# Attention: row maxima turned on VectorE, softmax totals inverted and spread by DMA, head outputs put in the last layer's order by DMA

## The reference

```
xd      = layernorm(x) @ W_down                      # 8 x 1024 x 256
keys, queries, values = per-head 16x16 products of xd, keys and queries scaled
attn    = softmax(queries @ keys^T over all 1024 keys)
out     = x + (attn @ values) @ W_unify + b_unify
```

## Time and profile before

| | |
|---|---|
| median of 3 runs | 2914.65 us |
| profiled execution, its own time / span | 2909.2 / 2907.5 us |
| TensorE busy (matmul) | 94% |
| VectorE / ScalarE / GpSimd busy | 74% / 63% / 21% |
| attention | about 640 to 2280 us of the span |
| mean granted TensorE clock | 0.968 of full |

### The profile page before, as it was taken

The page is one execution under the profiler, slowest core; times in us unless marked ns, Lnnn a source line. Parts: engine busy times, 40 slices in busy tenths (PEclk is TensorE's granted clock), DMA queues, the critical chain, the costliest instruction groups (busy, mean ns, idle before and its releaser), DMA issues. The chain is left out here.

```text
span 2907.5 us, 48802 instructions
## 1 busy us (share of the span) xinstructions
PE 2719.2 (94%) x17073; PEld 1648.7 (57%) x17073; DVE 2138.9 (74%) x3424; ACT 1838.3 (63%) x3473; POOL 600.8 (21%) x562
## 2 busy tenths in 40 slices
PE   5899999967999999999999999999999579999997
PEld 4799998853334334333343343333433369999886
DVE  6655456647899888898998988888896565554674
ACT  5444455633777777777777777777777444444564
POOL 3354114521100101001001001010000145421353
PEclk9899999977999999999999999999999899999998
DMA  5211113414123132131231321312210512111342
GB/s 171 66 43 49 52 52 104 137 51 79 24 52 70 32 61 52 38 61 36 48 74 32 58 55 29 70 36 43 51 41 2 161 39 80 49 43 43 97 135 66
DMA packets 159666, 180.66 MB, mean 62 GB/s; under 512 B 31816, under 2 KB 129296, under 8 KB 159504
## 3 DMA queue, kind: packets, MB, share of 16 engines
q1 hardware_dynamic: 151312, 167.99, 23.6%
q0 software_dynamic: 8192, 10.57, 1.2%
HBM read 96.46 MB, written 30.49 MB: 44 GB/s over the span
## 5 line engine op out<-in xcount | busy, mean ns | idle before, releaser
L1524 DVE TENSOR_REDUCE at_mxc<-at_pb 128x2 f32<-128x1024 f32 x1024 | 1219.6, 1219 | 157.7 <-PE at_pb L1341 150.0
L1454 ACT ACTIVATE at_ex<-at_pd 128x512 f32<-128x512 f32 x2048 | 1091.3, 599 | 361.6 <-PE at_pd L1352 355.1
L768 DVE TENSOR_TENSOR f_ml_hl<-f_ml_h,f_ml_hh 128x512 fp32r<-128x512 f32 (+1 forms) x384 | 289.2, 754 | 419.6 <-ACT f_ml_hh L844 416.7
L1352 PE MATMUL at_pd<-at_qa,at_ka 50*128 50x512 f32 x2048 | 587.5, 469 | 3.3 <-ACT at_ex L1454 2.5
L1352 PEld LDWEIGHTS at_pd<-at_qa,at_ka 50*128 50x128 f32 x2048 | 266.7, 185 | 539.5 <-issue 297.5
L1361 PE MATMUL at_po<-at_ex,at_va 128*32 128x512 f32 x4096 | 547.2, 606 | 0.2 <-ACT at_ex L1454 0.2
L841 ACT ACTIVATE f_ml_h<-f_ml_pL,b1T 128x512 f32<-128x512 f32 (+1 forms) x384 | 244.3, 636 | 449.8 <-PE f_ml_pL L895 444.3
L1341 PE MATMUL at_pb<-at_ka,at_qa 48*128 48x512 f32 x2048 | 437.6, 451 | 17.3 <-DVE at_mxc L1524 9.2
L910 PE MATMUL f_ml_pA<-f_wh,f_ml_hh 128*128 128x256 f32 (+1 forms) x1408 | 408.9, 290 | 0.1
L913 PE MATMUL f_ml_pA<-f_wh,f_ml_hl 128*128 128x256 f32 (+1 forms) x1408 | 401.3, 285 | 0.0
L912 PE MATMUL f_ml_pA<-f_wl,f_ml_hh 128*128 128x256 f32 (+1 forms) x1408 | 401.3, 285 | 0.0
(11 more groups left out here) (129 smaller groups left out, 2660.7 us busy)
## 6 DMA issues: line engine op xcount, KB each, us to landing
f_wraw<-in_L_ffn_w SPq DMA_DIRECT2D x128, 256.0 KB, 2.7
at_qa<-at_parts SPq DMA_DIRECT2D x384, 64.0 KB, 2.4
at_ka<-at_parts SPq DMA_DIRECT2D x384, 64.0 KB, 2.4
f_ro_xr<-in_L_attn_x SPq DMA_DIRECT2D x16, 512.0 KB, 3.6
f_ml_xr<-in_L_attn_x SPq DMA_DIRECT2D x16, 512.0 KB, 3.8
x<-f_ml_yo SPq DMA_DIRECT2D x16, 512.0 KB, 3.6
at_xr<-x SPq DMA_DIRECT2D x16, 512.0 KB, 4.4
at_xres<-x SPq DMA_DIRECT2D x8, 1024.0 KB
```

Source lines behind the costliest of these rows:

```text
L768: eng.tensor_tensor(hl[h % RING][:, 0:w], h32[h % 2][:, 0:w], hh[h % RING][:, 0:w].bitcast(F32), ALU.subtract).then_inc(s_lo.sem, 1)
L1352: eng.matmul(pd[n % RING][:, :], ka[g][rows, p, kt * P:(kt + 1) * P], qa[g][rows, qh, p, :], start=True, stop=True).then_inc(s_full.sem, 1)
L1454: eng.activation(ex[t % 2][:, j, :], pd[n % RING][:, :], ACT.Exp).then_inc(s_free[n % RING].sem, 1)
L1524: eng.tensor_reduce(mxc[:, t // NT, kh, t % NT::NT], pb[kh][:, :].rearrange("p (e k) -> p e k", e=2), AX.X, ALU.max).then_inc(s_mx.sem, 1)
```

## The change

1. **Maxima.** `mx` is gone from TensorE and ScalarE. The reductions write negated maxima; VectorE combines the two key halves, rounds them (`both_halves`), takes the rest (`rest`) and turns 32x32 blocks (`turn`). `load_maxima` is now: write the result to DRAM (`mscr`), wait for its landing, read it into `qa` by two DMAs.
2. **Totals and outputs.** `f` and `aT` are gone. `heads_out`: four DMAs spread the four totals' rows of `os` over 128 partitions by sixteen columns (`tot`), four more bring the head outputs to `aT`. VectorE inverts `tot` (`reciprocals`); `totals_out` writes it to DRAM (`rscr`), waits, and reads it back repeated over 64 partitions (`den`). GpSimd multiplies (`divide`).
3. **Places.** All four `u` of a batch stand in group 0 of the next one (steps 2, 3, 9, 12); before, two stood in group 3. LEAD is 13. The two load semaphores of a group are one, but for group 0.

```diff
-    LEAD = 12
+    LEAD = 13
-            table = {1: ("f", 1), 9: ("f", 0), 4: ("mx", 1), 12: ("mx", 0)}
+            table = {}
+            if g == 0 and prev:
+                table.update(zip((2, 3, 9, 12), OUT(0) + OUT(1)))
             if g == 3 and last:
-                del table[12]
...
+                table.update(zip((14, 15), OUT(0)))
...
+            def load_maxima(b, g, qh):
+                h = half(b, g, qh)
+                eng.wait_ge(s_nm.sem, s_nm.at(4 * h + 4))
+                to = mscr[g, qh, :, :, :, :, :].rearrange("m e c k i -> k (m e c) i")
+                eng.dma_start(to, mT[:, qh, :]).then_inc(s_ms.sem, 16)
+                eng.wait_ge(s_ms.sem, s_ms.at(16 * (h + 1)))
+                for e in range(2):
...
+                    eng.dma_start(to.bitcast(F32), src).then_inc(s_mr[h % 2].sem, 16)
+            def heads_out(ring, b, g, qh, read):
+                eng.wait_ge(s_o.sem, s_o.at(half(b, g, qh) + 1))
+                for j in range(GH):
...
+                    eng.dma_start(tot[VW * j:VW * (j + 1), :],
...
+                for j in range(GH):
...
+                    eng.dma_start(aT[r0:r0 + HS, qh, g // 2, :], os_[r1:r1 + HS, :]).then_inc(s_nd.sem, 16)
+            def totals_out(b, g, qh):
+                eng.wait_ge(s_rc.sem, s_rc.at(2 + h + 1))
+                eng.dma_start(rscr[g, qh, :, :].rearrange("j (x y) -> (j x) y", y=HS), tot[:, :]).then_inc(s_rs.sem, 16)
+                eng.wait_ge(s_rs.sem, s_rs.at(16 * (h + 1)))
...
+                src = rscr[g, qh, :, :].unsqueeze(1).broadcast_to([GH, HS, NQ])
+                eng.dma_start(den[r0:r0 + HS * GH, qh, :], src).then_inc(s_nd.sem, 16)
...
+                    if t == NT:
+                        heads_out(self.ring, b, g, 0, self.read[0])
+                    if t == NT + 3:
+                        totals_out(b, g, 0)
+                    if t == 0 and (b or g):
+                        heads_out(self.ring, *before(b, g), 1, self.read[1])
+                    if t == 3 and (b or g):
+                        totals_out(*before(b, g), 1)
+                    if t % NT == 4 and coming_half(t, g, last):
+                        load_maxima(*half_ahead(b, g, t))
...
+                                  AX.X, ALU.max, negate=True).then_inc(s_mx.sem, 1)
+                eng.wait_ge(s_nd.sem, s_nd.at(16 * (GH + 1) * half(b, g, t // NT)))
                 eng.tensor_copy(os_[:, :], po[:, :]).then_inc(s_o.sem, 1)
+            def reciprocals(b, g, qh):
+                eng.wait_ge(s_td.sem, s_td.at(16 * GH * (half(b, g, qh) + 1)))
+                eng.reciprocal(tot[:, :], tot[:, :]).then_inc(s_rc.sem, 1)
...
+            def divide(b, c, f):
+                eng.wait_ge(s_nd.sem, s_nd.at(16 * (GH + 1) * (half(b, 2 * c + 1, f) + 1)))
+                eng.tensor_tensor(aT[:, f, c, :], aT[:, f, c, :], den[:, f, :], ALU.mult).then_inc(s_dv.sem, 1)
```

More of the change, by code:

```diff
@@ L1156, in attention @@
              (3, 9), (3, 13), (0, 1), (0, 5), (0, 7), (0, 9), (0, 13), (1, 1)))}
-        splits = lambda task: task[0] in ("qk", "mx")
+        splits = lambda task: task[0] == "qk"
+        landed = lambda g, p: s_ld[0] if (g, p) == (0, 0) else s_ld[1 + g]
+        loads = lambda g, b: (ULOADS if g else ULOADS // 2) * 2 * 16 * b
+        half = lambda b, g, qh: 2 * unit(b, g) + qh
         unit = lambda b, g: 4 * b + g
         next_unit = lambda b, g: (b, g + 1) if g < 3 else (b + 1, 0)
+        before = lambda b, g: (b, g - 1) if g else (b - 1, 3)
+        half_ahead = lambda b, g, t: (b, g, 1) if t < NT else (*next_unit(b, g), 0)
+        coming_half = lambda t, g, last: t < NT or g < 3 or not last
         class Place:
@@ L1188, in __init__ @@
                         self.phase(do, b, b % 2, g, prev=b > 0, last=b == NBAT - 1)
-                do.end([self.place(task, NBAT - 1, 1, 3) for task in [("f", 1)] + OUT(1)])
+                do.end([self.place(task, NBAT - 1, 1, 3) for task in OUT(1)])
             def place(self, task, b, par, g):
@@ L1212, in phase @@
                         a = self.place(task, b + 1, 1 - par, g)
[L1213 to L1217, removed]
+                    elif task and task[0] == "u" and g == 0:
                         a = self.place(task, b - 1, 1 - par, g)
@@ L1223, in phase, with units_landed @@
                     do.step(b, par, g, t, coming, tiles, done, a, side, ahead, last)
+        def units_landed(eng, b, c):
+            for g, p in ((0, 0), (0, 1), (1, 0)) if c == 0 else ((2, 0), (3, 0)):
+                eng.wait_ge(landed(g, p).sem, landed(g, p).at(loads(g, b)))
         block = ctx.enter_context(nc.Block())
@@ L1228, in _ @@
         def _(eng):
-            for s in (*s_xr, *(x for two in s_ld for x in two), *s_mr, s_xl, *s_st):
+            for s in (*s_xr, *s_ld, *s_mr, s_ms, s_td, s_rs, s_nd, s_xl, *s_st):
                 s.open(eng)
@@ L1318, in step @@
                         store_out(self.ring, a)
+                        self.read[a.at[0]] = a.n
                 def end(self, sides):
-                    for a in sides[3:]:
+                    heads_out(self.ring, NBAT - 1, 3, 1, self.read[1])
+                    totals_out(NBAT - 1, 3, 1)
+                    for a in sides:
                         store_out(self.ring, a)
@@ L1335, in for_max @@
                 qh, p, qt = t // NT, t % NT // 4, t % 4
-                if t in (0, NT // 2) and kh == 0:
-                    eng.wait_ge(s_ld[g][p].sem, s_ld[g][p].at(16 * ULOADS * (b + 1)))
+                if kh == 0 and (t == 0 or g == 0 and t == NT // 2):
+                    eng.wait_ge(landed(g, p).sem, landed(g, p).at(loads(g, b + 1)))
                 eng.wait_ge(s_mx.sem, s_mx.at(2 * (ST * unit(b, g) + t) + kh - 1))
@@ L1603, in first @@
                             both_halves(0, 0, t // NT)
-                        if t == NT:
-                            side_out(self.ring, a)
+                            rest(0, 0, t // NT)
+                            turn(0, 0, t // NT)
                 def lead(self, b, g, tiles):
@@ L1612, in step @@
                         maximum(*ahead, 0)
+                    if t % NT == 3 and coming_half(t, g, last):
+                        rest(*half_ahead(b, g, t))
                     if a:
@@ L1617, in step @@
                         if ahead[2] % NT == NT - 1:
-                            both_halves(ahead[0], ahead[1], ahead[2] // NT)
+                            both_halves(*half_ahead(b, g, t))
+                    if t % NT == 3 and coming_half(t, g, last):
+                        turn(*half_ahead(b, g, t))
                     if t % NT == NT - 1:
                         values_out(b, g, t)
+                    if t == NT + 2:
+                        reciprocals(b, g, 0)
+                    if t == 2 and (b or g):
+                        reciprocals(*before(b, g), 1)
                     if g == 0 and not last and t < 8:
```

180 lines of the change are left out of this document (82 added, 98 removed).

## The result

The changed kernel takes 2957.64 us (median of 4 runs, 2952.32 to 2962.77), the kernel before 2912.9 in the same comparison: 1.0147 times as long, 95% interval 1.0121 to 1.0172. It is slower; 2899 and faster was forecast, and the range ended at 2944. The profiled execution has a span of 2950.6 us, 43.1 more than before, of which 39.7 lie before the next layer's first load (2319.59 us, 2279.92 before), so in attention: up to it both kernels run alike, and the first reduction starts at 673.92 us, 675.02 before.

A forecast was written before the change was run, and what follows sets the result against it. TensorE's row of work was taken to set seven halves of eight, VectorE the first; 2909.2 - 62.2 + 2.3 + 8 + 36.4 = 2893.7, with the runs' median 5.4 above: 2899 us, range 2862 to 2944.

The forecast's parts named there:

- TensorE's side tasks: f, mx and aT in TensorE's steps: removing them takes 131 x 0.475 = 62.2 us off the path.
- The half with layer norm: First half of a batch, set by VectorE (26.62 of 26.90 us busy): no gain from the change.
- SyncE's queue: DMA issue in groups 2 and 3: 86 us of queue against 85 of TensorE; groups 0 and 1 keep up.
- The end: From attention's last copy to the next layer's first load: 23 us instead of 15.2, +8 us.
- the sum without its waits: Whole kernel if SyncE's queue hides everything: 2899 - 36 = 2863 us.
- the term of 36.4 us: TensorE's waits for maxima in groups 2 and 3: 5.2 us per batch in seven batches.
- 1 us more for the maxima's way: Sensitivity of TensorE's waits in groups 2 and 3: they would grow to 9.5 us per batch.
- Rival C: Maxima's way 1.6 us longer per half, from den's few engines or a late scattered write: 2941 us; chance 0.20.
- Rival D: VectorE becomes the bound in plain halves, 0.5 us per half over 50 halves: 2924 us; chance 0.12.
- The start: One step more of maxima ahead of the first exponential, two reductions: +2.3 us.

The follow-up runs named there:

- e4: Kernel before with the maxima's part of the change alone; totals, outputs, f, aT and u as before: 2886.01 us, 0.9926.
- e5: e1 with the four DMAs that bring the head outputs to aT issued by GpSimd instead of SyncE: 2862.98 us, 0.9819.
- e2: Changed kernel with den read as one row of totals repeated 64 times instead of four rows sixteen times: 2908.15 us, 0.9993.
- e1: Changed kernel with totals_out issued behind load_maxima instead of ahead of it: 2883.16 us, 0.9909.
- e8: e4 with eight small DMAs and their landing ahead of the maxima's write in group 2's second half of every batch: 2911.77 us, 0.9998.
- e3: Changed kernel with four extra score matmuls per step without for_max in the last batch's last group: 2944.17 us, 1.0129.
- e6: e5 with the extra score matmuls of e3 in the last batch's last group: 2856.46 us, 0.9799.
- e7: Changed kernel with den's transfer issued a second time, into DRAM, ahead of the maxima's write: 2999.3 us, 1.0294.

## Why the prediction was wrong

**Right in mechanism.** TensorE's side tasks set the halves, and one is worth 0.48 to 0.52 us (e4). The half with layer norm gains nothing (26.42). SyncE's queue binds in groups 2 and 3 and not in 0 and 1. TensorE waits for the maxima most in second halves (2.04 and 5.72 us idle in the batch shown, against 2.0 and 3.2). The end fits (22.8 against 23), and so does the sum without its waits (e5).

**The step that failed** is the term of 36.4 us, the waits that the account of SyncE's queue in groups 2 and 3 gave. They are 61 us, 8.7 per batch instead of 5.2. Two prices in that account were too low. `load_maxima` holds SyncE for 4.1 us instead of 3.5, because `den`'s transfer stands just ahead of its write (e2). And the totals' write, priced at 2.3 us, lands after 2.5 to 4.0 behind `xr`; behind `xres`, priced at 3.8, after 3.1 to 5.1. With both, SyncE comes later to each half: in group 3's second half the maxima's write is issued 18.9 us after the first step and not 16.4. The maxima's own way from there was priced nearly right: 5.1 us, against 5.0 to 5.8 up to TensorE's next matmul, the write longer and the read shorter than in the sum. That `xr` and `xres` hold up the totals' write is read from where they stand; no run moved them. But in e1, where `den` is out of the way, the write to `mscr` still takes 2.2 to 4.2 us to the read in just these two halves, and 2.0 in the other halves of groups 2 and 3. And in batch 6, which loads no `xr`, that landing takes 2.15 us, and TensorE is idle for 2.35 us and not 4.0 to 5.7.

Two small errors in the working changed nothing: a copy of maxima is 0.70 us by the earlier trace rows, not 0.65 (the eight issues of `heads_out` took 5.0 to 5.6 us in this batch, for 5.1), and "1 us more for the maxima's way" gives 8.8 us per batch by the prediction's own steps, not 9.5.

**Rival C**, with 0.20 of the chance and 2941 us, came nearest, and part of that is luck. Its mechanism is there: `den` stands just ahead, and e2 measures 1.3 us for it where C had 1.6. But C put this on top of a way that was already priced 1 us too long (4.0 to 4.4 us in e2, 5.1 in the sum), so its 11.2 us of waits per batch are more than the 8.7 found. I had weighed against C that landings hardly grow from 8 to 256 KB; none of those rows is a broadcast read of four rows, or a small write just behind one.

**The term missing from every case, C's too,** is TensorE's clock. Every term took TensorE at full clock, as in the earlier trace rows. The 61 us of waits came with 86 us of lengthening; the other 25 are put down to the clock by difference, and e8 shows the same third. And the last half lost 10 us with no wait at all. The change took `f` and `aT` from its steps, which hold no `for_max` either; such steps lost the clock in three runs of five (e3), so these 10 us could also have stayed away. From 2899: 50 more in groups 2 and 3 (half of it waits, half the clock) and 11 in the last half give 2960; 2957.6 was measured.

**Not decided by VectorE.** Rival D fell: plain halves take 20.9 us with all their reductions, in e1, e5 and e6. The start cost what was forecast: from the first reduction to the first exponential it is 29.4 us instead of 26.7, 2.7 more for 2.3.

## What to carry to other kernels

A wait for a DMA's landing inside an in-order queue of DMAs costs all that stands behind it; put what is needed soonest first (e1: 74 us from moving two calls), and count what is left on the queue (e5: 20 more). Work taken off the engine that sets the pace gains only as long as the queue that replaces it has time in the very stretch where its product is due. And look at the granted clock behind each wait and in stretches that were made thin: here it cost as much as the waits that the account of the queue had missed (25 us each), and 10 us more at the end.

## What the runs showed of the hardware that I had not expected

- The shape of a broadcast read decides how late it lands: 128 KB as four rows sixteen times took 3.7 us (median) from issue to its reader, as one row 64 times 2.9; a small write 0.5 to 0.6 us behind it took 3.5 us against 2.2 to its landing (e2).
- TensorE's clock fell to the lower level in steps without `for_max` and side tasks, with no wait ahead of it: the longest idle time of TensorE in the 11 us before was 0.45 us. In e2 and e7 the same steps kept the full level.
- In e8 the clock stayed up behind three waits of 1.6 to 1.7 us, and fell behind two of 1.5 us.
- GpSimd issued four plain DMAs in 1.99 us (e5), SyncE the same four in 2.49 (changed kernel).
